# A field-interaction tower on one core: layer 1's fourth unit in halves, the block matrix on ScalarE, accumulator banks by parity

## The reference, cut to what matters

```python
x_vec = input                                    # (batch, 64, 16)
for W, b in params:                              # three layers, 128 outputs each
    z = jnp.einsum('bhd,bfd->bhfd', x_vec, input)
    B, h, f, d = z.shape
    z = z.reshape(B, h * f, d)
    x_vec = jnp.einsum('oc,bcd->bod', W, z) + b[None, :, None]
    outs.append(x_vec.sum(axis=2))
```

## Time and profile before

| | |
|---|---|
| median of 3 runs | 1167.39 us (1166.23 to 1167.61) |
| profiled execution, its own time | 1163.56 us |
| its span, first to last instruction | 1161.6 us |
| mean granted TensorE clock | 0.997 |
| PE busy | 1098.8 us (95%) |
| DVE busy | 1011.0 us (87%) |
| POOL busy | 905.4 us (78%) |
| ACT busy | 688.7 us (59%) |
| chain that ended last | PE 84% |

### The profile page before, as it was taken

How to read it: one execution, slowest core, us unless ns; L and a number is a source line. 1 busy time by engine, 2 the same in 40 slices (tenths; PEclk the granted TensorE clock), 3 DMA queues, 4 the chain that set the end, 5 groups by cost and what they waited for, 6 DMA issues and landing times.

```text
span 1161.6 us, 13994 instructions
## 1 busy us (share of the span) xinstructions
PE 1098.8 (95%) x4276; PEld 744.5 (64%) x4276; DVE 1011.0 (87%) x670; ACT 688.7 (59%) x712; POOL 905.4 (78%) x403
## 2 busy tenths in 40 slices
PE   0479999999999999999999999999999999999998
PEld 0246666666666666667666666666676666666696
DVE  4599899999999999989999999999899999998452
ACT  5365466665656656665566666566656566566443
POOL 6469989888988888888988888888889887567000
PEclk9989999999999999999999999999999999999999
DMA  6642415334262525143352524252442525142891
GB/s 239 185 124 66 114 49 153 93 100 145 67 169 75 152 64 161 47 150 94 81 156 73 164 79 136 72 159 57 126 118 79 155 75 159 57 148 88 292 355 41
DMA packets 101789, 142.87 MB, mean 123 GB/s; under 512 B 11746, under 2 KB 55010, under 8 KB 98947
## 3 DMA queue, kind: packets, MB, share of 16 engines
q1 hardware_dynamic: 93570, 140.42, 39.3%
q0 software_dynamic: 8192, 2.11, 2.3%
HBM read 114.96 MB, written 27.53 MB: 123 GB/s over the span
## 4 chain that ended last, share of the span: by engine, by line
PE 84%; POOL 7%; DVE 3%; issue 3%; ACT 2%; DMA 1%; SPq 0%; ACTq 0%; DVEq 0%
PE acc L1110 49%; PE acc L1104 25%; POOL emb L574 3%; POOL z_lo L583 3%; PE z_ps L1251 3%; PE turn_gram_ps L1179 3%; PE z_ps L1241 1%; DVE z L654 1%; DVE z_float L654 1%; ACT x L901 1%; PE turn_gram_ps L1166 1%; DVE z_ps L660 1%; PE acc L1136 1%; DVE z_lo L666 1%; DMA land<-x_scratch 0%
## 5 line engine op out<-in xcount | busy, mean ns | idle before, releaser
L583 POOL TENSOR_TENSOR z_lo<-z,z_hi 128x2048 fp32r<-128x2048 f32 x143 | 659.8, 4615 | 104.4 <-ACT z_hi L864 102.2
L1104 PE MATMUL acc<-z_float,w_sb 128*128 128x512 f32 x768 | 348.7, 600 | 56.8 <-DVE z_float L654 43.2
L1110 PE MATMUL acc<-z_hi,w_hi 128*128 128x512 f32 x896 | 378.3, 422 | 2.5 <-POOL z_lo L583 1.6
L1110 PE MATMUL acc<-z_hi,w_lo 128*128 128x512 f32 x896 | 353.7, 395 | 0.0
L1110 PE MATMUL acc<-z_lo,w_hi 128*128 128x512 f32 x896 | 353.3, 394 | 0.0
L864 ACT ACTIVATE z_hi<-z 128x2048 fp32r<-128x2048 f32 x144 | 275.2, 1911 | 60.5 <-DVE z L654 60.5
L574 POOL DMA_INDIRECT emb<-in_tables,rows_chunk x256 | 245.3, 958 | 63.8 <-issue 56.4
L1104 PEld LDWEIGHTS acc<-z_float,w_sb 128*128 128x128 f32 x768 | 145.7, 192 | 213.0 <-issue 199.0
L873 ACT ACTIVATE z_hi<-z_ps 128x1024 fp32r<-128x1024 f32 x160 | 164.5, 1028 | 127.1 <-PE acc L1110 72.7
L666 DVE TENSOR_TENSOR z_lo<-z_ps,z_hi 128x1024 fp32r<-128x1024 f32 x160 | 194.5, 1216 | 32.5 <-ACT z_hi L873 32.5
L654 DVE TENSOR_TENSOR z<-operand_even,x_shift 128x2048 f32<-128x2048 f32 x80 | 182.9, 2286 | 38.6 <-PE acc L1110 16.2
(11 more groups left out here) (117 smaller groups left out, 631.9 us busy)
## 6 DMA issues: line engine op xcount, KB each, us to landing
land<-x_scratch SPq DMA_DIRECT2D x128, 256.0 KB
land<-x_scratch SPq DMA_DIRECT2D x128, 128.0 KB
x_shift<-x_scratch SPq DMA_DIRECT2D x16, 1024.0 KB, 5.8
gram_scratch<-gram SPq DMA_DIRECT2D x32, 512.0 KB, 6.5
x_shift<-x_scratch SPq DMA_DIRECT2D x16, 768.0 KB, 8.1
z_float<-gram_scratch SPq DMA_DIRECT2D x7, 1024.0 KB, 9.5
x_scratch<-emb SPq DMA_DIRECT2D x32, 192.0 KB, 2.8
x_shift<-gram_scratch SPq DMA_DIRECT2D x6, 1024.0 KB, 6.4
```

The costliest lines, as they stand in the source:

```text
L583: pool.tensor_tensor(z_lo[:, slot], z[:, slot], z_hi[:, slot].bitcast(F32), ALU.subtract).then_inc(subtracted, 1)
L1104: mm = pe.matmul(acc[:, :], weights[:, tile0 + q, :], z_float[:, g.float_slot(pos), q, :], start=start and q == 0, stop=stop and q == QUAD ...
L1110: mm = pe.matmul(acc[:, :], w[:, tile, :], zz[:, slot, q, :], start=False, stop=stop and n == 2)
```

## The change: what it does

- Layer 1's unit m3 becomes a halves unit. PE does 12 float32r matmuls for it in two halves where it did four float32 ones. DVE forms it in two halves and makes two low parts; ACT rounds two more halves. It uses the same `z_ps` and the same `HALVES_SLOT` as m2, right after it. Its weights move from the plain to the split ones.
- DVE's list in `layer1_middle` becomes: half m2 first, `split_square`, its low part, half m2 second, `sum2` of the chunk before, its low part, half m3 first, d1, its low part, half m3 second, d0, its low part. The operand banks for d are released by the halves of m2 and m3.
- `form_blocks` on DVE goes. ACT makes the four copies one by one (`form_block`), each a copy of 128x256 from PSUM scaled by a column of the mask; in a round they stand behind `take_x2`, behind the rounding of a3, and around that of b1. At the end all four stand before the last `take_x2`.
- `acc1` and `acc2` become `acc[0]` and `acc[1]`: both layers of a chunk use the bank of its parity. Layer 1 of a chunk waits for x2 of the chunk two before, layer 2 for x1 of its own chunk.
- The scratch for the gathers' descriptors shrinks from 8192 to 4096 bytes. PE waits for all split weights before layer 1 of chunk 1, not after.

```diff
-L1_SPLIT = 2 * QUAD
+L1_SPLIT = SPLIT_UNITS * QUAD
-L1_PLAIN, L2_PLAIN = 2 * QUAD, L2_GROUPS * QUAD
+L1_PLAIN, L2_PLAIN = QUAD, L2_GROUPS * QUAD
...
-        acc1 = ps("acc1", [P, COLS])
-        acc2 = ps("acc2", [P, COLS])
+        acc = [ps("acc_even", [P, COLS]), ps("acc_odd", [P, COLS])]
...
-            def layer1_middle(c):
-                layer1(c, 2, half=0)
-                layer1(c, 3)
-                split_half(layer1_group(c), 0)
-                layer1(c, 2, half=1)
+            def layer1_middle(c, *between):
+
+                g = layer1_group(c)
+                for n, (pos, half) in enumerate(((2, 0), (2, 1), (3, 0), (3, 1))):
+                    layer1(c, pos, half=half)
+                    if n < len(between):
+                        between[n]()
+                    split_half(g, half, pos)
...
-                form_blocks(prev)
                 layer2_middle(c, 1)
                 layer1(nxt, 1)
                 split_half(layer2_group(c, 1), 1)
-                sum2(prev)
                 layer1(nxt, 0)
-                split_square(nxt)
-                layer1_middle(nxt)
-                layer2(c, 2, 1)
-                split_half(layer1_group(nxt), 1)
-                layer2(c, 2, 0)
+                layer1_middle(nxt, lambda: split_square(nxt), lambda: sum2(prev),
+                              lambda: layer2(c, 2, 1), lambda: layer2(c, 2, 0))
...
             def released_by_layer1(g, bank):
-                return (halves_formed, g.count(2, 2)) if bank == 0 else (formed, g.count(3, 3))
+                return halves_formed, g.halves(2 + 2 * bank)
...
-            def round_half(g, half):
-                act.wait_ge(halves_formed, g.count(2, half + 1))
-                if not g.is_first:
+            def round_half(g, half, pos=2):
+                act.wait_ge(halves_formed, g.halves(2 * (pos - 2) + half + 1))
+                if not (g.is_first and pos == 2):
                     if half == 0:
-                        act.wait_ge(half_used, g.count(1))
+                        act.wait_ge(half_used, g.halves_units(pos - 2))
+                    elif pos == 3:
+                        act.wait_ge(used, g.count(4, 3))
                     else:
-                        act.wait_ge(used, g.count(4, -1))
+                        act.wait_ge(used, g.count(4, 0 if g.layer1_at(1) else -1))
...
+            def form_block(c, b):
+
+                if b == 0:
+                    act.wait_ge(x0_turned, c.count(1, 1))
+                    if not c.is_(0):
+                        act.wait_ge(gram_done, c.count(HALVES))
+                act.activation(blocks[:, :, b, :], x0t_ps[:, 0:BLOCKS, :], ACT.Copy,
+                               scale=mask_sb[:, b:b + 1]).then_inc(block_ready, 1)
...
                 round_half(m, 1)
+                round_half(m, 0, 3)
                 to_bank(d, 1, 1, released_by_layer1(m, 1))
+                round_half(m, 1, 3)
                 round_unit(d, 1)
...
             def layer1(c):
                 g = layer1_group(c)
-                if not c.is_(0):
-                    pe.wait_ge(x1_ready, c.count(1))
+                if not (c.is_(0) or c.is_(1)):
+                    pe.wait_ge(x2_ready, c.count(1, -1))
...
-                halves_unit(g, acc1, QUAD)
-                float_unit(g, acc1, w0_sb, QUAD, pos=3, stop=True)
+                halves_unit(g, acc[c.par], QUAD)
+                halves_unit(g, acc[c.par], 2 * QUAD, pos=3, stop=True)
...
-                        if i == 0 and not c.is_(0):
-                            pe.wait_ge(x2_ready, c.count(1))
-                        float_unit(g, acc2, w1_sb, QUAD * i, start=i == 0)
+                        if i == 0:
+                            pe.wait_ge(x1_ready, c.count(1, 1))
+                        float_unit(g, acc[c.par], w1_sb, QUAD * i, start=i == 0)
...
-    nc = bacc.Bacc("TRN2", target_bir_lowering=False, num_devices=1, dynamic_dma_scratch_size=8192)
+    nc = bacc.Bacc("TRN2", target_bir_lowering=False, num_devices=1, dynamic_dma_scratch_size=4096)
```

More of the change, by code:

```diff
@@ L155, in units, with products, halves, halves_units @@
         return self.chunk.count(2 * GROUPS - 1, 2 * groups - layer1 + more)
+    def products(self, more=0):
+        groups, layer1 = self.before()
+        return self.chunk.count(3 * GROUPS - 1, 3 * groups - layer1 + more)
+    def halves(self, more=0):
+        groups, layer1 = self.before()
+        return self.chunk.count(2 * GROUPS + 2, 2 * groups + 2 * layer1 + more)
+    def halves_units(self, more=0):
+        groups, layer1 = self.before()
+        return self.chunk.count(GROUPS + 1, groups + layer1 + more)
     def unit_slot(self, pos):
@@ L392, in load_x0 @@
                 if not (c.is_(0) or c.is_(1)):
-                    waits.append((halves_formed, Group(c.plus(-2), 4).count(2, 2)))
+                    waits.append((halves_formed, Group(c.plus(-2), 4).halves(2)))
                 load_copies(c, 1, 5, x0_loaded, *waits)
@@ L505, in _ @@
             sp.dma_start(dense_sb, dense).then_inc(top_in, 16)
-            sp.wait_ge(halves_formed, Group(end.plus(-1), 4).count(2, 2))
+            sp.wait_ge(halves_formed, Group(end.plus(-1), 4).halves(2))
             sp.wait_ge(x0_turned, CHUNKS - 1)
@@ L589, in round_ @@
                     for pos in (1, 3):
-                        if not (pos == 3 and Group(c, j).is_layer1):
+                        if pos == 1 or not Group(c, j).is_layer1:
                             low_part(Group(c, j), pos)
@@ L813, in _ @@
             split_half(layer2_group(end, 3), 1)
-            form_blocks(end)
             sum2(end)
@@ L1042, in _ @@
                     take_x2(prev)
+                    for b in range(TILE_B):
+                        form_block(prev, b)
                 if i == 1:
@@ L1056, in _ @@
             take_gram(prev, 1, 1)
+            for b in range(TILE_B):
+                form_block(end, b)
             take_x2(end)
```

122 lines of the change are left out of this document (55 added, 67 removed).

## The result

The change makes the kernel slower by 8.7%, by the mechanism that was forecast and by more than its price: 1268.17 us lies outside the forecast's own range of 1230 to 1262, and inside the range for 8 in 10, 1215 to 1282.

A forecast was written before the change was run, and what follows sets the result against it. PE was taken as the bound, busy 95% in rounds of 64.35 us. 73 us for 14 rounds, 6 startup, 0.2 at the end, less 0.5, make 79; with the 1167.4 median, 1246 us (own range 1230 to 1262; 8 in 10: 1215 to 1282).

The forecast's parts named there:

- The hand-over of the slot: Layer 1, m3 right behind m2: PE stands 1.14 us, then 3.09, a round while the one slot refills.
- second wait: Before m3's second half: PE stands 3.09 us, since z_ps frees late and d0 precedes the low part.
- The gram's wait: Behind layer 1: PE waits 1.91 us more a round for ACT to take the gram's second bank.
- The rival without it: PE finds the gram's bank already taken: 27 us less, 1219 us; chance 0.15.
- The x2 wait: Layer 1: with banks by parity PE's wait for x2 goes, 0.5 us less a round.
- the split unit: m3 on PE: as float32r halves it takes 2.79 us for 3.43, saving 0.64 in each of 16 chunks.
- the blocks: Four copies on ACT: 1.4 us of ACT a round, nothing on the path, 0.2 us at the end.
- the scratch: Smaller scratch for the gathers' descriptors: costs nothing if it is enough.
- POOL's rival: Smaller scratch holds up gathers by 0.3 us each, POOL becomes the bound: 56 us more, 1300 us; chance 0.06.
- The startup: Before the rounds: hand-overs and lost lead in the first chunks cost 6 us (0 to 9).
- The clock: Rival: PE's new waits let its clock fall each round, 2.3 us each, 32 more, 1278 us; chance 0.13.
- PEclk under 1.00 in the rounds: Granted PE clock below full in the rounds, named as a sign that the forecast is wrong.

The follow-up runs named there:

- E1: Changed kernel with m3 a float unit again; banks by parity, blocks on ACT and small scratch stay: 1159.81 us, 0.9948 of before.
- E5: Changed kernel with PE doing m1 between m2 and m3, and split_square ahead of m2's first half: 1232.91 us, 1.0588 of before.
- E10: E9 with ACT also taking the gram's second bank ahead of rounding d3: 1226.72 us, 1.0528 of before.
- E12: Kernel before with only the accumulators' banks by parity: 1157.32 us, 0.9945 of before.
- E2: Changed kernel with split_square moved back ahead of the first half of m2: 1257.35 us, 1.0788 of before.
- E8: Kernel before with only split_square moved behind the first half of m2: 1169.11 us, 1.0037 of before.
- E4: Changed kernel with PE doing m1 between m2 and m3, other engines' lists unchanged: 1250.22 us, 1.0697 of before.
- E6: E2 with m3's halves in a slot of their own, the one d3 uses next: 1238.60 us, 1.0638 of before.
- E9: E6 with ACT rounding d1 ahead of the bank copy and m3's second half: 1236.19 us, 1.0614 of before.
- E7: E2 with ACT taking the gram's second bank ahead of rounding d3 and of x1: 1246.41 us, 1.0699 of before.
- E11: E2 with ACT rounding d1 earlier, m3 still in the slot shared with m2: 1249.67 us, 1.0728 of before.

## Why the prediction was right, and where its 22 us are

The forecast was 1246 us with 1215 to 1282 around it; measured are 1268.17. By the profiled executions it is 1264.0 for 1242.5, 21.5 us more.

*The hand-over of the slot.* Right, to 0.01 us at both restarts; E1 shows that m3 in halves carries the whole loss. Its second wait, of 2.9 us, is that of a half on its way through `z_ps` and DVE's list, as the prediction's own steps have it, and stands in E5 and E10 without the slot's part; the name that I gave to both fits only the first. The reasoning that held was to count from one instant of PE through ACT and DVE with everything that stands ahead on each list, the bank copy and d0 included. What I took as 3.09 of standing reads 2.92 plus a first record of 0.50; the price was the same.

*The gram's wait.* Right in place and size (1.91 forecast, 1.90 at 616.54), though in ten rounds the slow clock fills most of it. The rival without it is out.

*The x2 wait, the split unit, the blocks, the scratch.* Right. E12: 0.5 us a round for the banks. E1: nothing for the blocks, whose copies take 0.47 to 0.50 us and start 0.36 apart, 1.4 in a round as taken; nothing for the scratch (the gathers 973 ns in the mean, 958 in rows 11). POOL's rival is out.

*The step that was missed in the rounds: `split_square`.* The diff moves it behind the first half of m2, and I gave that no term, because in the old trace it is a 0.69 us instruction. What it costs depends on what POOL does at that time. It explains most of the 12.0 us that the rounds have over the forecast: four of the six rounds above 69.83 (72.18, 71.41, 72.24, 72.22) hold a square of over 5 us and are 10.2 us longer together than four of 69.46. The other two are the clock's (below), though the last of them, 71.09, holds a square of 3.29 us. E2 gives 8.4 us back. E8 shows one such meeting in a kernel that has nothing else of the change.

*The startup, 15.4 for 6.* Its first two low parts, timeline of POOL, show where. Before, then after:

```profile
64.18 4.67 POOL L583 TENSOR_TENSOR z_lo<-z,z_hi 128x2048 fp32r<-128x2048 f32 x1 [17.28 <-ACT z_hi L864]
...
77.59 4.54 POOL L583 TENSOR_TENSOR z_lo<-z,z_hi 128x2048 fp32r<-128x2048 f32 x1 [3.88 <-ACT z_hi L864]
```
```profile
69.42 4.50 POOL L592 TENSOR_TENSOR z_lo<-z,z_hi 128x2048 fp32r<-128x2048 f32 x1 [22.09 <-ACT z_hi L851]
...
92.98 4.54 POOL L592 TENSOR_TENSOR z_lo<-z,z_hi 128x2048 fp32r<-128x2048 f32 x1 [13.93 <-ACT z_hi L851]
```

From the second of these low parts to the first `turn_x0` both kernels take the same, 52.81 and 52.83 us. So 5.24 us arise ahead of the first and 10.15 between the two. And there the rows of ACT and DVE of the changed kernel are

```profile
50.97 0.60 ACT L829 ACTIVATE operand_odd<-land 128x512 f32<-128x512 f32 x1 [8.04 <-DMA land<-x_scratch]
...
74.56 0.69 ACT L883 ACTIVATE x<-acc_even,bias_sb 128x512 f32<-128x512 f32 x1 [5.23 <-DVE z_sq L724]
```
```profile
70.16 4.31 DVE L724 TENSOR_TENSOR z_sq<-x,z_sq 64x512 fp32r<-64x512 f32 x1
...
76.72 1.22 DVE L675 TENSOR_TENSOR z_lo<-z_ps,z_hi 128x1024 fp32r<-128x1024 f32 x1 [2.25 <-issue]
```

Of the 10.15, 3.5 are the square again: it meets the first low part, and x1 and the rounding of m2 stand behind it (from the first unit formed to m2's first low part 12.2 us for 8.7). The other 6.6 are four halves in a row through one `z_ps` (76.72 to d1's form at 88.67 is 11.95, before 5.31); that is the part that I had forecast, with a fair size. Of the 5.24, about 1 is the same for chunk 0, and some 4.2 is a copy that landed late: ACT's at 50.97 stands at 45.03 before. It is no property of the change. E1 to E4, which ran on one chip, all have it at 50.9 to 51.6, E1 included; E5 to E12, on another, at 43.5 to 45.7, whatever the kernel. Why it landed later there was not tried.

*The clock.* I gave it 0.13 as a rival and put it at nothing in the sum, and I named PEclk under 1.00 in the rounds as a sign of being wrong. The sign came: 0.97 in the 14 rounds. The Trainium skill's rule that a loop which waits in every turn pays in every turn (TensorE: Matmul & The Clock Gate, section HAM oscillation) has the trace behind it in most rounds: one float unit after the two waits reads up to 5.29 us for 3.59. But the price is not the rival's 2.3 us a round: in nine of the ten slow rounds PE still waits for the gram behind the slow unit. Two rounds do pay, with 2.6 us together. In that of 70.41 the float unit takes 5.29 us (539.92) and the gram does not wait. In that of 71.09 the waits are the usual ones (1.03, 2.92, 1.89) and the clock falls behind the last of them, where nothing covers it. Windows behind the gram's matmul, in the round of 69.45 (333.10) and in this one (1108.37):

```profile
333.10:338.10 5.00, 5.00 (x25) 3.92 (x26) 5.00 (x4) 3.12 (x3) 4.82 (x3) 1.00 0.55 162
```
```profile
1108.40:1113.40 5.00, 5.00 (x18) 3.79 (x19) 5.00 (x4) 3.09 (x3) 4.89 (x2) 0.66 0.56 161
```

From there to `turn_x0` it is 21.45 and 23.02 us. The same fall behind the gram's wait costs 1.5 us in one round of E2, in five of E4, in 11 of E6 and in 12 of E9, and 3.0 in one more each of E6 and E9. So the clock was a small term in the changed kernel and a large one in those that were to mend it. In the startup the float units read 5.24 and 5.10 us with PEclk at 0.50, which looks like the missing time; E7 has 3.67 for both and needs the same 76.4 us from its first low part to `turn_x0` (65.23 to 141.59, here 69.42 to 145.81). There the slow clock cost nothing.

**What stays open.** A kernel in which m3 has its own slot does not come back to 64 us: its rounds are the sum of PE's two waits and the slow stretch behind the gram's (E9). Why DVE reaches m3 without a lead is argued, not shown. E9 excludes POOL, the gathers and the landed copies there, and E11 the order of d1 with the shared slot; E6 excludes the slot as the whole of it; E10 excludes the gram alone. What is left is VectorE's list: m3 in halves brings it 2.4 us more a round, of its 4.4 to spare, and four halves in a row, each of which waits for ACT's rounding of the one `z_ps`. A second `z_ps`, or d0 behind m3's last low part, would tell; neither was tried.

## What to carry to other kernels

A single buffer is free of cost as long as other work lies between its two uses; before a second unit is put right behind the first, count the refill from the instant the consumer lets go, through each engine's list, with everything queued ahead. An instruction that is moved is not worth its old duration at its new place: look at what the other elementwise engine does at that time. And a wait that ends latest hides others; take the hidden ones (here the clock, POOL's low part, VectorE's list) as the price that remains when it is removed, before promising its full length.
